# Experts' up product from rounded halves: weights split block by block, low parts shared by GpSimd and VectorE

## The reference, cut to what matters

```python
he = einsum('nd,edh->enh', xf, expert_w1) + expert_b1    # 512 -> 768: the up product
g, u = clip(he[..., ::2]), clip(he[..., 1::2])           # gate and up are interleaved
te = g * sigmoid(g * alpha) * gate_scale * (u + up_shift)
oe = einsum('enh,ehd->end', te, expert_w2) + expert_b2   # 384 -> 512: the down product
out = x + shared(xf) + sum over experts of cw[:, e] * oe # cw: the two chosen experts' weights
```

## Time and profile before

| what | value |
|---|---|
| time of the runs (median of 3) | 908.85 us (907.89 to 909.83) |
| time of the profiled execution | 910.05 us |
| its span, first to last instruction | 908.3 us |
| PE busy, share of the span | 811.4 us, 89% |
| DVE busy | 485.9 us, 53% |
| ACT busy | 250.2 us, 28% |
| POOL busy | 126.6 us, 14% |
| up product of the experts, line 1224 | 155.9 us of PE, 448 records |
| down product of the experts, line 1272 | 78.6 us of PE, 168 records |

### The profile page before, as it was taken

How to read it: one execution, slowest core, us unless ns; L and a number is a source line. 1 busy time by engine, 2 the same in 40 slices (tenths; PEclk the granted TensorE clock), 3 DMA queues, 4 the chain that set the end, 5 groups by cost and what they waited for, 6 DMA issues and landing times.

```text
span 908.3 us, 12470 instructions
## 1 busy us (share of the span) xinstructions
PE 811.4 (89%) x3696; PEld 583.8 (64%) x3697; DVE 485.9 (53%) x949; ACT 250.2 (28%) x502; POOL 126.6 (14%) x186
## 2 busy tenths in 40 slices
PE   4679699999999986948999958989999999999993
PEld 2555588888888863626888846887655555555551
DVE  6899481441341387899024685896343443434341
ACT  2455241331341103515221313421021222212121
POOL 2000000000000120000000500212123333333321
PEclk9985699999999995979999968979999999999997
DMA  2600000000000010000101102004698859663542
GB/s 112 205 1 2 1 1 1 0 1 1 1 1 1 29 40 9 1 1 1 47 1 53 58 1 92 22 1 176 218 355 248 297 136 367 167 180 57 135 92 32
DMA packets 32156, 71.34 MB, mean 79 GB/s; under 512 B 4254, under 2 KB 4504, under 8 KB 32110
## 3 DMA queue, kind: packets, MB, share of 16 engines
q1 hardware_dynamic: 25838, 56.04, 17.1%
q0 software_dynamic: 6272, 14.68, 8.1%
HBM read 96.53 MB, written 12.72 MB: 120 GB/s over the span
## 4 chain that ended last, share of the span: by engine, by line
PE 70%; DVE 17%; DMA 6%; issue 3%; ACT 2%; SPq 1%; ACTq 0%; DVEq 0%; POOL 0%; POOLq 0%
PE PS L994 20%; PE PS L1224 14%; PE PS L1024 9%; PE PS L1272 7%; PE PS L1117 5%; PE PS L1063 3%; DMA WB<-in_w 3%; PE PS L925 3%; DMA X<-in_x 3%; PE PS L1257 2%; DVE XN L1343 1%; PE PS L1208 1%; DVE ET L1396 1%; DVE ET L1391 1%; ACT CTR L693 1%
## 5 line engine op out<-in xcount | busy, mean ns | idle before, releaser
L994 PE MATMUL PS<-CTR,YH 125*128 125x500 f32 (+1 forms) x480 | 164.1, 357 | 2.3 <-DVE YL L1526 2.3
L994 PE MATMUL PS<-CTR,YL 125*128 125x500 f32 (+1 forms) x480 | 163.6, 356 | 0.0
L1224 PE MATMUL PS<-WB,YF 128*128 x448 | 155.9, 492 | 0.1
L1224 PEld LDWEIGHTS PS<-WB,YF 128*128 128x128 f32 x448 | 80.9, 190 | 65.7 <-issue 20.7
L994 PEld LDWEIGHTS PS<-CTR,YH 125*128 125x128 f32 x480 | 91.5, 191 | 15.5 <-DVE YL L1526 2.6
L994 PEld LDWEIGHTS PS<-CTR,YL 125*128 125x128 f32 x480 | 91.5, 191 | 13.1
L925 PE MATMUL PS<-ET 125*128 125x130 f16 x494 | 66.4, 302 | 21.1 <-DVE ET L1401 17.2
L1272 PE MATMUL PS<-WB,YF 128*128 x168 | 78.6, 605 | 1.6 <-DMA WB<-in_w 0.9
L925 PEld LDWEIGHTS PS<-ET 125*128 125x128 f16 x494 | 43.2, 128 | 45.0 <-DVE ET L1401 22.2
L1553 DVE TENSOR_TENSOR ZL<-PS,ZH 128x500 fp32r<-128x500 f32 (+1 forms) x36 | 21.1, 592 | 90.1 <-ACT ZH L745 90.1
L648 POOL DMA_INDIRECT out<-YF,dest_i x28 | 44.6, 1591 | 73.5 <-ACT YF L891 48.4
(11 more groups left out here) (363 smaller groups left out, 1369.0 us busy)
## 6 DMA issues: line engine op xcount, KB each, us to landing
WB<-in_w SPq DMA_DIRECT2D x28, 1536.0 KB
WB<-in_w SPq DMA_DIRECT2D x28, 768.0 KB
WB<-in_b SPq DMA_DIRECT2D x28, 384.0 KB
X<-in_x SPq DMA_DIRECT2D x1, 2500.0 KB
xn_dram<-XN SPq DMA_DIRECT2D x1, 2500.0 KB
out<-X SPq DMA_DIRECT2D x10, 250.0 KB
WNEXT<-in_W SPq DMA_DIRECT2D x2, 1024.0 KB, 10.1
SR<-in_sw SPq DMA_DIRECT2D x1, 1536.0 KB, 7.8
```

The lines of the kernel that those rows point to most:

```text
L994: mm = nc.tensor.matmul(dest, lhs, rhs, start=(t == 0 and h == 0), stop=(t == NT - 1 and h == 1))
L1224: mm = nc.tensor.matmul(PS[:, 2 * k + h, 0:INTER], xgt[:, k, f, :], WB[:, bass.ds(off + (f * H2 + h * INTER), INTER)], start=(f == 0), sto ...
```

## The change

The up product takes the rounded form. Rows and first matrix are both split, the matrix anew for every block:

- `rows_hi` (ACT) copies the transposed rows to `XGH`, rounded; `rows_lo` (DVE) makes the rest, `XGL`. They take the place of `rows_copy`.
- `split_hi` (ACT) copies the block's first matrix from `WB` to `W1H`, rounded, in two halves of 128 x 1536. `split_lo` subtracts: the first half on DVE, the second on POOL, both into `W1L`. `W1H` and `W1L` have two buffers each. Those of odd blocks lie in the memory of `X` (and a little past it), so their first use waits for the stores of `X`: `out_head` counts the first six stores, `out_stored` the other four.
- `up` makes 24 matmuls of 128 x 384 in place of 8, and waits for the low parts of each half.
- The order of the stage is turned so that rows and weights are ready one block earlier; `AHEAD` (gathers ahead of scatters) goes from 3 to 4. On POOL the second low part of each block stands behind a gather and a scatter.

```diff
-AHEAD = 3
+AHEAD = 4
+HEAD = 6
...
-                sp.dma_start(out[t * NP:(t + 1) * NP, :], X[0:NP, t, :]).then_inc(out_stored, 16)
+                sp.dma_start(out[t * NP:(t + 1) * NP, :], X[0:NP, t, :]).then_inc(out_head if t < HEAD else out_stored, 16)
...
@@ POOL, behind the gathers of blocks 0 to AHEAD-1 @@
-            gather(0, 1, AHEAD)
-            scatter(0, 0)
-            with pool.Fori(2, NB // 2) as i:
+            def split_lo(k, b):
+                off = pool.value_load(eb_i[0:1, 1, bass.ds(b, 1)], min_val=0, max_val=(NWB - 1) * WBUF)
+                cols = slice(INTER, H2)
+                pool.wait_ge(w1_hi, b * 2 + 2)
+                raw = WB[:, bass.ds(off, FT * H2)].rearrange("p (f n) -> p f n", f=FT)
+                pool.tensor_tensor(W1L[k][:, :, cols], raw[:, :, cols], f32(W1H[k][:, :, cols]), ALU.subtract
+                                   ).then_inc(w1_lo2, 1)
+            def pair(i):
+                gather(i, 0, i * 2)
+                scatter(0, i * 2 - AHEAD)
+                split_lo(1, i * 2 - 1)
+                gather(i, 1, i * 2 + 1)
+                scatter(1, i * 2 + 1 - AHEAD)
+                split_lo(0, i * 2)
+            split_lo(0, 0)
+            pool.wait_ge(out_stored, 16 * (NT - HEAD))
+            split_lo(1, 1)
+            split_lo(0, 2)
+            pair(AHEAD // 2)
+            with pool.Fori(AHEAD // 2 + 1, NB // 2) as i:
                 with pool.If(i < last + 1):
-                    gather(i, 0, i * 2)
-                    scatter(1, i * 2 - AHEAD)
-                    gather(i, 1, i * 2 + 1)
-                    scatter(0, i * 2 + 1 - AHEAD)
+                    pair(i)
...
@@ ACT @@
+            def rows_hi(k, b):
+                act.wait_ge(xt_ps, b + 1)
+                nc.scalar.copy(XGH[:, k, :, :], PS[:, 4, :].rearrange("p (f n) -> p f n", f=FT)).then_inc(xgt_hi, 1)
+            def split_hi(i, k, b, h):
...
+                act.wait_ge(w1_in[k], i * 32 + 32)
+                if not (isinstance(b, int) and b < 2):
+                    act.wait_ge(hb_ready, b - 1)
...
+                nc.scalar.copy(W1H[k][:, :, cols], raw[:, :, cols]).then_inc(w1_hi, 1)
+            def pair(i):
+                rows_hi(0, i * 2)
+                sigmoid(0, i * 2 - 2)
+                split_hi(i, 0, i * 2, 0)
+                if not (isinstance(i, int) and i < 2):
+                    result(1, i * 2 - 3)
+                split_hi(i, 0, i * 2, 1)
+                turn_t(0, i * 2 - 2)
...
+            split_hi(0, 0, 0, 0)
+            split_hi(0, 0, 0, 1)
+            act.wait_ge(out_head, 16 * HEAD)
+            split_hi(0, 1, 1, 0)
+            split_hi(0, 1, 1, 1)
+            rows_hi(0, 0)
+            rows_hi(1, 1)
...
@@ PE @@
             def turn_rows(i, k, b):
                 pe.wait_ge(gathered[k], i * 16 + 16)
+                if not (isinstance(b, int) and b < 1):
+                    pe.wait_ge(xgt_ready, b)
...
+                    cols = slice(h * INTER, (h + 1) * INTER)
+                    pe.wait_ge(w1_lo2 if h else w1_lo, b + 1)
                     for f in range(FT):
-                        mm = nc.tensor.matmul(PS[:, 2 * k + h, 0:INTER], xgt[:, k, f, :],
-                                              WB[:, bass.ds(off + (f * H2 + h * INTER), INTER)],
-                                              start=(f == 0), stop=(f == FT - 1))
+                        for j, (x, wt) in enumerate(((XGH, W1H), (XGL, W1H), (XGH, W1L))):
+                            mm = nc.tensor.matmul(PS[:, 2 * k + h, 0:INTER], x[:, k, f, :], wt[k][:, f, cols],
+                                                  start=(f == 0 and j == 0), stop=(f == FT - 1 and j == 2))
...
+            def pair(i):
+                turn_rows(i, 0, i * 2)
+                if not (isinstance(i, int) and i < 2):
+                    down(i - 2, 1, i * 2 - 3)
+                up(1, i * 2 - 1, lambda: turn_act(0, i * 2 - 2))
+                turn_rows(i, 1, i * 2 + 1)
+                down(i - 1, 0, i * 2 - 2)
+                up(0, i * 2, lambda: turn_act(1, i * 2 - 1))
...
@@ DVE @@
+            def rows_lo(k, b):
+                dve.wait_ge(xgt_hi, b + 1)
+                v.tensor_tensor(XGL[:, k, :, :], PS[:, 4, :].rearrange("p (f n) -> p f n", f=FT), f32(XGH[:, k, :, :]),
+                                ALU.subtract).then_inc(xgt_ready, 1)
...
-            for t in range(1, NT - 1):
+            for t in range(1, 5):
                 z_add(t, t)
-            rows_copy(0, 0)
+            split_lo(0, 0)
+            z_add(5, 5)
+            for t in range(6, NT - 1):
+                z_add(t, t)
+            rows_lo(0, 0)
             z_add(NT - 1, NT - 1)
-            rows_copy(1, 1)
-            units(0, 0, lambda: None)
-            units(1, 1, lambda: rows_copy(0, 2))
+            rows_lo(1, 1)
+            dve.wait_ge(out_stored, 16 * (NT - HEAD))
+            split_lo(1, 1)
+            def pair(i):
+                units(0, i * 2 - 2, lambda: rows_lo(0, i * 2))
+                split_lo(0, i * 2)
+                units(1, i * 2 - 1, lambda: rows_lo(1, i * 2 + 1))
+                split_lo(1, i * 2 + 1)
```

More of the change, by code:

```diff
@@ L654, in _ @@
             last = last_pair(pool)
-            gather(0, 1, AHEAD)
-            scatter(0, 0)
-            with pool.Fori(2, NB // 2) as i:
-                with pool.If(i < last + 1):
-                    gather(i, 0, i * 2)
-                    scatter(1, i * 2 - AHEAD)
-                    gather(i, 1, i * 2 + 1)
-                    scatter(0, i * 2 + 1 - AHEAD)
-            ending = pool.value_load(eb_i[0:1, 3, 1:2], min_val=SURE - AHEAD, max_val=NB - AHEAD)
-            for j in range(AHEAD):
-                scatter((j + 1) % 2, ending + j)
+            def split_lo(k, b):
[13 more added lines that the diff above has]
+            split_lo(0, 0)
+            pool.wait_ge(out_stored, 16 * (NT - HEAD))
+            split_lo(1, 1)
+            split_lo(0, 2)
+            pair(AHEAD // 2)
+            with pool.Fori(AHEAD // 2 + 1, NB // 2) as i:
+                with pool.If(i < last + 1):
+                    pair(i)
+            end = ending(pool)
+            scatter(0, end)
+            split_lo(1, end + 3)
+            for j in range(1, AHEAD):
+                scatter(j % 2, end + j)
             pool.wait_ge(scattered, pool.to_reg(last * 32 + 32))
@@ L885, in sigmoid, with result @@
                                      ).then_inc(gate_sig, 1)
-            def result(i, k, b, first=False):
+            def result(k, b):
                 act.wait_ge(y_done, b + (EARLY + 1))
-                if not first:
+                if not isinstance(b, int):
                     act.wait_ge(scattered, act.to_reg(b * 16 - 16))
+                elif b >= 2:
+                    act.wait_ge(scattered, b * 16 - 16)
                 nc.scalar.activation(yo[:, k, :], PS[:, 6 + k, :], ACT.Copy,
@@ L895, in _ @@
             last = last_pair(act)
[L896 to L900, removed]
-                with act.If(i < last + 1):
[L902 to L910, removed]
@@ new lines, in pair @@
+            def pair(i):
[6 more added lines that the diff above has]
+                turn_t(0, i * 2 - 2)
+                rows_hi(1, i * 2 + 1)
+                sigmoid(1, i * 2 - 1)
+                split_hi(i, 1, i * 2 + 1, 0)
+                result(0, i * 2 - 2)
+                split_hi(i, 1, i * 2 + 1, 1)
+                turn_t(1, i * 2 - 1)
@@ new lines, in _ @@
+            split_hi(0, 0, 0, 0)
[5 more added lines that the diff above has]
+            rows_hi(1, 1)
+            pair(1)
+            pair(2)
+            with act.Fori(3, NB // 2) as i:
+                with act.If(i < last + 1):
+                    pair(i)
+            end = ending(act)
+            sigmoid(0, end + 2)
+            result(1, end + 1)
+            turn_t(0, end + 2)
@@ L915, in _ @@
+            sigmoid(1, end + 3)
+            result(0, end + 2)
+            turn_t(1, end + 3)
+            result(1, end + 3)
         @block.tensor
@@ L1306, in _ @@
             shared_down(NT - 1)
-            pe.wait_ge(xgt_ready, 1)
             turn_rows(0, 1, 1)
-            up(0, 0, 0, None)
+            up(0, 0, None)
             pe.wait_ge(z_added, EARLY)
[L1311 to L1315, removed]
-                with pe.If(i < last + 1):
[L1317 to L1329, removed]
+            def pair(i):
[6 more added lines that the diff above has]
+                up(0, i * 2, lambda: turn_act(1, i * 2 - 1))
+            pair(1)
+            pair(2)
+            with pe.Fori(3, NB // 2) as i:
+                with pe.If(i < last + 1):
+                    pair(i)
+            end = ending(pe)
+            down(last - 1, 1, end + 1)
+            up(1, end + 3, lambda: turn_act(0, end + 2))
+            down(last, 0, end + 2)
+            turn_act(1, end + 3)
+            down(last, 1, end + 3)
         @block.vector
```

56 lines of the change are left out of this document (35 added, 21 removed).

## The result

The changed kernel takes 965.46 us in the median of 4 runs (961.96 to 967.19), beside 909.34 us (907.89 to 910.51) for the kernel before on the same chip: 1.0613 times the time, 95% interval 1.0577 to 1.0649. The forecast of 919 had the sign and missed the size: 56 us slower, not 10. The profiled execution took 964.27 us, its span 962.6.

The account below looks back on a forecast made before the run. POOL's cycle, with scatter landings, was taken to bound the changed kernel. The opening loses 17 us and the pace gives back 6.6, so 10.4 us on 908.85 makes 919.3; range 902 to 936.

Parts of the forecast that it names:

- PE's gain: On PE, up's 384-column matmuls take 0.176 us each, so a block needs 7.75 us, one us less.
- a lower clock: A lower granted clock behind PE's waits would push the time up; no size was given.
- The opening: In the first blocks, waits for X's stores and split_lo delay up(1) from 658.25 to 675.2 us, costing 17 us.
- Both are hidden by PE in the steady state: Per steady block, ACT's 5.7 us and DVE's 6.1 us of work fit under PE's 7.75 us.
- 25 x 8.15 + 13.8: Steady stage: 25 POOL cycles of 8.15 us plus 13.8 us for long scatter landings, 217.6 us to split_lo(27).
- Rival 3: In every block, DVE's split and products and POOL's split hold each other off: 21 us more, 940; chance 0.17.
- The rule quoted from the Trainium skill: A two-SBUF-input VectorE instruction and an SBUF-reading GpSimd one exclude each other; the second waits for the whole first.
- POOL's queue: Between two scatters, POOL's scatter, split_lo, gather, index copies and waits sum to 8.08 us, 8.15 with seams.
- The landings: In POOL's loop, ten of 24 scatter landings outlast 7.13 us of other work; their excesses cost 13.8 us.

Follow-up runs that it names:

- the kernel with both limits eased: Against the changed kernel, the clips read PSUM and POOL's two index copies stand ahead of its subtraction: 947.29 us, 1.0446 times the kernel before.

## Why the prediction was wrong

**PE's gain: right.** 0.175 us a matmul against 0.176. PE wasn't the bound, though, and its own time a block came out longer than the 7.75 us of the sum: it is busy for 8.31 us a block (216.07 us in 677.83 to 941.21), at a mean granted clock of 0.95. The prediction had named a lower clock and left it unpriced.

**The opening: right, but for the clock.** It cost 19.3 us for 17, in the steps that were worked out. The 2.3 us between arose at up(0)'s second half. POOL's low part let it start at 667.05 in place of 666.2. After 3.06 us without work PE then ran its 12 matmuls in 3.6 us, to the transposes at 670.61, where 2.13 had been reckoned. The granted clock was 0.59 of full from 667 to 670.7: most of these matmuls start 0.32 us apart, at the lower of the two levels (1.2 GHz), and the last ones 0.17 apart, at the higher (2.4 GHz). This is the term left unpriced. The run with the rows moved shows that the last store and the hold between the two splits set the opening's length, not the wait for the sixth store.

**The step that failed** is "Both are hidden by PE in the steady state", with the sum built on it, 25 x 8.15 + 13.8. It gives up(27) at 897.3; it ended at 941.1 (938.98 + 2.10 in the chain). Of the 43.8 us, 2.3 come from the opening and the rest from the pace. ACT's and DVE's sums were compared with PE's 7.75 as if their work were free to move. It isn't: clip, sigmoid, high half and result copy form one chain in ACT's and DVE's queues, and POOL's scatter and subtraction close it. With the hold, the loop takes 9.6 to 9.8 us in a quiet stretch (858 to 907 us), 1.5 more than 8.15, which is 40 us over 26 blocks.

**The cause was named and then mis-applied.** Rival 3, "The exclusion costs in every block", had 0.17 and 940. It looked for operations with two SBUF inputs (the split and the two products), found that they fitted one after the other, and passed the clip by. The rule quoted from the Trainium skill, "SBUF — State Buffer", section "Who interferes with whom", was read by half: the same section lists tensor_scalar among the operations that can take the ports shared with GpSimd, when its operands meet certain conditions. The trace agrees that the clip is held, 3.17 us against 0.50.

**POOL's queue: right in kind, mis-sized.** Its 8.08 measured 9.31 and 9.36 us where it waited for nothing. The hold works both ways: DVE's split stretches POOL's index copies, 1.20 us in place of 0.18. Even without the clip's loop the stage would have been slow: removing either limit alone gave at most 3 us, removing both gave 18.

**The landings: about right.** The wait that was priced is there: POOL's index copy waits for the landing of the scatter before, 9.1 us in seven waits from 684 to 935 us, where 13.8 was forecast. By the pace it is much the same: that of 10.13 stands some 0.4 above the quiet 9.7, 11 us over 26 blocks. That this is all due to landings is argued from the waits, not shown; the run with earlier gathers shows 8.4 us of that kind.

**What stays open:** why one block takes about 12 us with the split on VectorE in every order tried, and the 23 us by which the kernel with both limits eased (947) is slower than the one without POOL's subtraction (924). Late gathers and landings are seen in its waits; how they share it with the product still held wasn't taken apart. Of the block of 12 us the traces show the place. It is block 26, the first behind the loop, and with earlier gathers PE stands still for 2.55 us ahead of its down product and DVE for 3.99 us ahead of its bias add, both put down to no wait at all ("issue"). So the traces put neither a landing nor the hold there; what keeps the engines isn't shown.

## What to carry to other kernels

Before work goes to an engine with time to spare, follow the queue around: an instruction that is hidden by its busy share can still close a loop through three in-order queues, and the loop's length, not any engine's sum, is the pace. Where two engines lock each other out, list every operation that runs beside the new one by where its operands lie, not only the likely ones. When an edit that should help does nothing, look for a second limit of the same length before the theory is thrown away: here only the two edits together moved the time.

## What was not expected of the hardware

A DVE tensor_scalar with one SBUF tensor in and SBUF out, at 0.47 to 0.52 us for 384 elements (the bias add, one input from PSUM, takes 0.96 for 768, the same rate), is held until a POOL tensor_tensor beside it has ended: 3.39 us in the block shown, 1.2 to 4.4 in the 24 blocks where the two overlap. The same operation read from PSUM isn't held, at 0.68 us, nor are the bias add (0.96) and, in the run with the clips from PSUM, rows_lo (0.68), each with one PSUM input and started inside the subtraction. The other way round, a POOL copy of one column took 1.20 us instead of 0.18 inside a DVE subtraction.
